# We's row in PSUM, and PE's side jobs behind each chunk's sums in a message-passing kernel on one Trainium2 core

## The reference

```python
xn = layernorm(x)
# 4 graph layers
for l in range(4):
    e   = edge_weight1 @ We[l] + be[l]              # (E,1) @ (1,D): one row We[l] times a number per edge
    m   = relu(h[src] + e)                          # a message per edge
    agg = segment_sum(m, dst, N)
    h   = ((1 + eps[l]) * h + agg) @ W1[l] + b1[l]
    h   = relu(batchnorm(h) * gamma[l] + beta[l])
    h   = relu(h @ W2[l] + b2[l])
# linear attention on the same xn
q, k, v = elu(xn @ Wq + bq) + 1, elu(xn @ Wk + bk) + 1, xn @ Wv + bv
kv = sum_s k v^T (per head);  z = 1 / (q . sum_s k)
mixed = (q kv z) @ Wp + bp
x = x + h + mixed
x = x + expert_ffn(layernorm(x))                    # top-1 of 8 experts
```

## Time and profile before

| what | value |
|---|---|
| median of 3 runs | 1772.68 us (1770.53 to 1775.09) |
| the profiled execution | 1772.85 us, of it 1771.1 us span |
| PE busy, x matmuls | 1462.0 us (83%) x6948 |
| DVE busy | 1310.3 us (74%) x2539 |
| POOL busy | 1081.7 us (61%) x1070 |
| ACT busy | 944.5 us (53%) x1086 |
| layer 0: start of POOL's first gather to the end of its last | 32.0 to 449.1 us |
| layer 1: relu of step 1 to relu of step 37 | 554.2 to 835.2 us |
| layer 2: the same | 933.0 to 1209.8 us |
| layer 3: the same | 1306.0 to 1583.8 us |

### The profile page before, as it was taken

The page is one execution under the profiler, slowest core; times in us unless marked ns, Lnnn a source line. Parts: engine busy times, 40 slices in busy tenths (PEclk is TensorE's granted clock), DMA queues, the critical chain, the costliest instruction groups (busy, mean ns, idle before and its releaser), DMA issues.

```text
span 1771.1 us, 22116 instructions
## 1 busy us (share of the span) xinstructions
PE 1462.0 (83%) x6948; PEld 645.9 (36%) x6948; DVE 1310.3 (74%) x2539; ACT 944.5 (53%) x1086; POOL 1081.7 (61%) x1070
## 2 busy tenths in 40 slices
PE   3767898867787888888888988889888898898797
PEld 2233344322333333333433333334433333334464
DVE  6788988978457887776586778776678878685634
ACT  3544544444245666665436667665456666673221
POOL 3777777777126777777047777773267777770033
PEclk8988999887999999999999999999999999999889
DMA  7776677677147777776257777783477777866343
GB/s 261 204 201 188 196 199 200 197 225 226 51 125 221 216 212 212 210 213 199 53 179 228 223 228 212 215 233 111 141 225 221 224 217 210 244 196 230 149 149 111
DMA packets 119094, 343.23 MB, mean 194 GB/s; under 512 B 20712, under 2 KB 24892, under 8 KB 118718
## 3 DMA queue, kind: packets, MB, share of 16 engines
q0 software_dynamic: 85248, 278.41, 55.0%
q1 hardware_dynamic: 32318, 60.78, 10.6%
q10 hardware_dynamic: 1408, 2.56, 0.4%
HBM read 323.61 MB, written 19.96 MB: 194 GB/s over the span
## 4 chain that ended last, share of the span: by engine, by line
PE 45%; DVE 16%; POOL 13%; ACT 12%; issue 8%; DMA 4%; DVEq 1%; POOLq 0%; ACTq 0%; SPq 0%
PE ps L1799 41%; POOL ring L817 13%; ACT ring L1593 10%; DVE ring L1006 8%; PE ps L1864 3%; DMA ring<-x_table,idxT 3%; DVE lg L1061 1%; DVE aggT L1421 1%; DVE onehot L1000 1%; DMA aggT<-pair_table,token_i 1%; DMA ring<-in_x 1%; DVEq L1048 0%; PE ps L2229 0%; DVE ring L940 0%; DVE aggT L1062 0%
## 5 line engine op out<-in xcount | busy, mean ns | idle before, releaser
L817 POOL DMA_INDIRECT ring<-x_table,idxT x1014 | 1039.3, 1025 | 514.4 <-issue 293.1
L1006 DVE SCALAR_TENSOR_TENSOR ring<-we_bc,wT,ring 128x512 f32<-128x512 f32 x1014 | 688.7, 747 | 63.6 <-DMA ring<-x_table,idxT 58.5
L1593 ACT ACTIVATE ring<-ring 128x3072 f32<-128x3072 f32 x161 | 444.7, 2762 | 282.9 <-DVE ring L1006 282.9
L1799 PE MATMUL ps<-ring,onehot 128*32 128x512 f32 x2028 | 360.2, 650 | 198.3 <-ACT ring L1593 194.5
L1639 ACT ACTIVATE zT<-ps 128x512 f32<-128x512 f32 x336 | 189.6, 601 | 145.6 <-PE ps L1799 142.7
L1799 PE MATMUL ps<-ring,zT 128*128 128x512 bf16 x1080 | 262.4, 382 | 0.8
L1799 PE MATMUL ps<-zT,xT 128*32 128x512 f32 (+2 forms) x752 | 256.5, 618 | 1.6 <-DVE mix L1195 1.6
L1061 DVE TENSOR_REDUCE lg<-ps 128x128 f32<-128x512 f32 x208 | 143.1, 688 | 118.0 <-PE ps L1864 72.2
L1799 PEld LDWEIGHTS ps<-ring,onehot 128*32 128x32 f32 x2028 | 72.3, 113 | 381.5 <-ACT ring L1593 242.9
L1799 PE MATMUL ps<-w,zT 128*125 128x512 f32 (+2 forms) x320 | 146.5, 621 | 20.2 <-ACT zT L1717 20.2
L1799 PE MATMUL ps<-aggT,w 128*128 128x512 f32 (+1 forms) x384 | 142.7, 522 | 6.9 <-DVE aggT L1062 3.6
(11 more groups left out here) (311 smaller groups left out, 1263.2 us busy)
## 6 DMA issues: line engine op xcount, KB each, us to landing
ring<-x_table,idxT POOLq DMA_INDIRECT x1014, 3.8
zT<-slot_table SPq DMA_DIRECT2D x36, 312.5 KB
w<-in_L_gnn_W SPq DMA_DIRECT2D x8, 1024.0 KB, 10.7
ring<-in_L_ffn_W SPq DMA_DIRECT2D x16, 512.0 KB, 9.8
x_table<-ring SPq DMA_DIRECT2D x24, 250.0 KB
x_table<-ring SPq DMA_DIRECT2D x9, 256.0 KB
stage<-in_x ACTq DMA_DIRECT2D x9, 256.0 KB
pair_table<-mix SPq DMA_DIRECT2D x9, 256.0 KB
```

The source lines that it names most:

```text
L817: gp.indirect_dma_start(out=to, out_offset=None, in_=table[:, :], in_offset=bass.IndirectOffsetOnAxis(ap=idx, axis=0)).then_inc(done, 16)
L1006: ins = v.scalar_tensor_tensor(out=at[:, u, :], in0=we_bc[:, :], scalar=wT[:, c, u:u + 1], in1=at[:, u, :], op0=ALU.mult, op1=ALU.add)
L1593: a.activation(at, at, ACT.Relu).then_inc(relu_done, 1)
L1799: return nc.tensor.matmul(o, lhsT, rhs, start=start, stop=stop)
```

## The change

1. **We's row in PSUM.** In layers 1 to 3 ACT copies `we_bc` into `ps[6]` (`terms_copy`, in `first_pieces`), in layer 0 into `ps[5]` at step 14, and DVE's edge terms read that bank in place of SBUF; layer 0 does so from step 15 on (`TERMS_FROM`).
2. **Banks.** `ps[6]` is no longer free in layers 1 to 3: the tiles rotate through two banks in all three layers (`TAKES = 2`), so `first` is 2 tiles in layers 2 and 3 too. `att` goes into `ps[7]`, the bank of `fold_picked`. The values of layer 0 go into `ps[7]`, kv into one bank as 8 matmuls of 64 rows x 65 columns a tile (4 of 129 columns before).
3. **Norms.** The attention's divisors are computed at the end of layer 0 (`norms`: 4 matmuls of 2 columns for each of 10 node tiles, at steps 47 to 51) and inverted there; `att` on DVE is one multiplication in place of two reciprocals and two.
4. **Order in layers 1 to 3.** On PE a step is now: `first` tiles, `group_sums` with `place_rows`, `fold_groups`, `fold_picked`, `later` tiles, side job, early sums. DVE and ACT look up the side job of step j-1 (`beside_of`), and DVE's `flush_picked` and statistics also come a step later. The fine steps are rearranged to match.

```diff
-    def takes(l):
-        return 2 if l == 1 else 3
+    TAKES = 2
...
-        return tiles[:takes(l)], tiles[takes(l):]
+        return tiles[:TAKES], tiles[TAKES:]
...
+    def beside_of(l, j):
+
+        return beside_at(l, j - 1)
...
+    TERMS_FROM = QS + 3
+    act_jobs[QS + 1].append(("terms", 0))
+
+    NORMS = ((46, range(0, 6)), (47, range(6, 7)), (48, range(7, 8)), (49, range(8, 9)), (50, range(9, NT)))
+    for at, tiles in NORMS:
+        pe_jobs[at] += [("norms", t) for t in tiles]
+    dve_jobs[51].append(("norms", 0))
...
+        def terms_bank(l):
+            return ps[6] if l in MIXED else ps[5]
...
+                terms = terms_bank(l) if l in MIXED or j >= TERMS_FROM else we_bc
+                if l not in MIXED and j == TERMS_FROM:
+                    v.wait_ge(terms_ready, 1)
                 for u in tiles:
-                    ins = v.scalar_tensor_tensor(out=at[:, u, :], in0=we_bc[:, :], scalar=wT[:, c, u:u + 1],
+                    ins = v.scalar_tensor_tensor(out=at[:, u, :], in0=terms[:, :], scalar=wT[:, c, u:u + 1],
                                                  in1=at[:, u, :], op0=ALU.mult, op1=ALU.add)
...
+            def terms_copy(l):
+
+                a.wait_ge(we_loaded, l * 16 + 16)
+                a.activation(terms_bank(l)[:, :], we_bc[:, :], ACT.Copy).then_inc(terms_ready, 1)
...
                 elif l in MIXED:
                     pe.wait_ge(pick_relu, QB[l + 1] * SW)
+                    pe.wait_ge(pick_out, QB[l + 1])
...
-                if at >= takes(l):
-                    pe.wait_ge(pick_relu, at - takes(l) + 1)
+                if at >= TAKES:
+                    pe.wait_ge(pick_relu, at - TAKES + 1)
...
+                    first, later = tiles_of(l, j)
+                    for T in first:
+                        take_rows(l, T)
+                    group_sums(l, j)
+                    for T in placed_at(l, j):
+                        place_rows(l, T)
+                    fold_groups(l, j - 1)
+                    if fold_at(j) is not None:
+                        fold_picked(l, fold_at(j))
+                    for T in later:
+                        take_rows(l, T)
                     beside(l, j)
                     early_sums(l, early_of(l, j))
-                    if fine_of(l, j) is not None:
-                        if l in MIXED and fold_at(j) is not None:
-                            fold_picked(l, fold_at(j))
-                        fine_sums(l, j)
-                        continue
-                    first, later = tiles_of(l, j) if l in MIXED else ([], [])
-                    for T in first:
-                        take_rows(l, T)
-                    if l in MIXED and fold_at(j) is not None:
-                        fold_picked(l, fold_at(j))
-                    group_sums(l, j)
-                    if l in MIXED:
-                        for T in placed_at(l, j):
-                            place_rows(l, T)
-                    fold_groups(l, j - 1)
-                    if l in MIXED:
-                        for T in later:
-                            take_rows(l, T)
...
+                if kind == "norms":
+                    r = rows(i)
+                    if i == 0:
+                        pe.wait_ge(v_ready, NT)
+                        pe.wait_ge(kvblk_ready, 1)
+                    for f in range(KD):
+                        at = i * NORM + f * 2
+                        ins = mm(v_bank[0:r, at:at + 2], mix[:, i, f * P:f * P + r], kvblk[:, f, P:], True, True)
                     ins.then_inc(nd_done, 1)
```

More of the change, by code:

```diff
@@ L191, in build_gps_block @@
                 order.append(("j", j - 2))
-            if l in MIXED and fold_at(j) is not None:
-                order.append(("q", fold_at(j)))
+            if l in MIXED and fold_at(j - 1) is not None:
+                order.append(("q", fold_at(j - 1)))
         assert len(order) == NC
@@ L1033, in add_fine @@
                     add_tiles(l, j, range(p * PAIR, (p + 1) * PAIR)).then_inc(last_summed, 1)
-                    if f == FINE - 1 and p == 1:
+                    if l in MIXED:
+                        if p == 0:
+                            flush(l, "j", j - 2)
+                            if f > 0:
+                                early_stats(l, early_of(l, j - 1))
+                        if p == 1:
+                            flush_picked(l, j)
+                            early_stats(l, early_of(l, j if f > 0 else j - 1))
+                    elif f > 0 and p == 1:
                         flush(l, "j", j - 2)
-                        if l in MIXED:
-                            early_stats(l, early_of(l, j))
                 if f == FINE - 1:
@@ L1040, in add_fine @@
                     flush(l, "j", j)
-                else:
+                elif l not in MIXED:
                     flush(l, "j", j - 2)
-                    flush_picked(l, j)
             def flush(l, kind, i):
@@ L1064, in flush_picked @@
             def flush_picked(l, j):
-                if l in MIXED and fold_at(j) is not None:
-                    flush(l, "q", fold_at(j))
+                if l in MIXED and fold_at(j - 1) is not None:
+                    flush(l, "q", fold_at(j - 1))
             def early_stats(l, e):
@@ L1093, in messages @@
             def messages(l):
-                v.wait_ge(we_loaded, l * 16 + 16)
+                if l in MIXED:
+                    v.wait_ge(terms_ready, l + 1)
+                else:
+                    v.wait_ge(we_loaded, 16)
                 if l in MIXED:
@@ L1110, in messages @@
                     beside(l, j)
-                    if l in MIXED:
-                        if ready_at(j) is not None:
-                            picked_ready(l, ready_at(j))
-                        if j < NJ[l] - 1:
-                            early_stats(l, early_of(l, j))
-                    else:
+                    if fine_of(l, j) is None or l not in MIXED:
                         early_stats(l, early_of(l, j - 1))
+                    if l in MIXED and ready_at(j) is not None:
+                        picked_ready(l, ready_at(j))
             def general(l):
@@ L1185, in beside @@
             def beside(l, j):
-                for kind, i in dve_jobs[j - 1] if l == 0 else beside_at(l, j):
+                for kind, i in dve_jobs[j - 1] if l == 0 else beside_of(l, j):
                     job(l, kind, i)
@@ L1720, in beside @@
             def beside(l, j):
-                for kind, i in act_jobs[j - 1] if l == 0 else beside_at(l, j):
+                for kind, i in act_jobs[j - 1] if l == 0 else beside_of(l, j):
                     if kind == "columns":
@@ L1854, in fine_sums @@
                 ins.then_inc(parts_done, 1)
-                fold_groups(l, j if f > 0 else j - 1)
+                if f > 0:
+                    fold_groups(l, j)
+                elif l not in MIXED:
+                    fold_groups(l, j - 1)
             def fold_groups(l, j):
@@ L2012, in key_value @@
                 for c in range(KD):
[L2013 to L2014 removed]
+                    for h in range(2):
+                        ins = mm(ps[6][h * HD:(h + 1) * HD, c * (HD + 1):(c + 1) * (HD + 1)], k_rows[0:r, c * P + h * HD:c * P + (h + 1) * HD],
+                                 v_rows[0:r, c, h, :], t == 0 and c == 0, t == NT - 1 and c == KD - 1)
                 ins.then_inc(kv_done, 1)
```

121 lines of the change are left out of this document (73 added, 48 removed).

## The result

The changed kernel takes 1825.06 us (median of 4 runs, 1824.27 to 1826.05) against 1773.88 us for the kernel before (median of 4, 1770.53 to 1779.96): a ratio of 1.029, 95% interval 1.027 to 1.032. It is slower by 51 us. The forecast was 1799 us and its range ended at 1811.

What follows compares the result with a forecast made beforehand. POOL was taken to bound layer 0, a loop of PE and ACT layers 1 to 3. Layer 0 -8, layer 1 +4.9, layer 2 +15.1 and layer 3 +14.0 made 1772.85 + 26 = 1799 us, range 1788 to 1811 (8 in 10: 1756 to 1811).

Steps and rivals of the forecast that it cites:

- What bounds the kernel: POOL's gathers pace layer 0 at 7.93 us a chunk; a loop of PE and ACT paces layers 1 to 3.
- The end of each layer (+2.8): Layers 1 to 3: last pair's relu 21.4 us after relu 37, against 18.64 before, +2.8 us a layer.
- Two banks in layers 2 and 3: Three steps take 23.10 or 24.41 us, not 23.64; first three +4.5 a layer, the rest +7.8 and +6.7.
- Rival B: Layers 2 and 3: the two banks cost nothing, each layer gives +5 to +6, 1781 us in all; chance 0.14.
- Fold_picked (+0.45 a turn): Layers 1 to 3: hidden before, it now stands inside the loop and adds 0.45 us a turn.
- Layer 0 (-8): Layer 0: 13 us gained by faster gathers less 5 us lost to the norms, -8 us in all.
- The gathers' pace: Layer 0 from step 15 on: 35 chunks at 7.57 us in place of 7.94, a gain of 13 us.
- the norms: End of layer 0: 10.5 us of PE work comes in, about 8 us are free, 5 us lost.
- Edge terms from PSUM at no price for DVE: DVE's edge terms: 745 ns with one operand in PSUM against 747 in SBUF, costed at 0.
- Rival C: Norms cost 10.5 us, or PSUM edge terms cost DVE 0.39 us a chunk where late: 1808 us; chance 0.09.
- Rival A: POOL paces layers 2 and 3 too, so faster gathers gain there: about 1744 us; chance 0.22.
- Rival D: Layer 0's gathers stay at 1.32 us, so layer 0 gives +5 in place of -8: 1812 us; chance 0.05.

Runs made afterwards that it cites:

- experiment 9: The changed kernel with DVE's statistics of the last early sums moved behind the last pair's edge terms: 1816.98 us, ratio 1.025.
- experiment 11: The changed kernel with one matmul in place of four in the early sum of step 37: 1814.97 us, ratio 1.023.
- experiment 12: The changed kernel with the edits of experiment 9 and experiment 11 together: 1799.06 us, ratio 1.015.
- experiment 6: The changed kernel with edge terms read from SBUF in layer 0 only: 1838.76 us, ratio 1.037.
- experiment 8: The changed kernel with layer 1 and layers 2 and 3 from step 34 in the old order, three banks and SBUF terms in layers 2 and 3: 1771.07 us.
- the executions listed above the experiments: Seven profiled executions sharing the changed kernel's layers 2 and 3: 290.3 us with one turn at the lower clock, up to 297.5 with four.
- experiment 1: The kernel before with two take banks in place of three in layers 2 and 3: 1793.95 us, ratio 1.012.
- experiment 3: The changed kernel with three take banks in layers 2 and 3 and edge terms from SBUF in layers 1 to 3: 1788.67 us, ratio 1.011.
- experiment 2: The changed kernel with `fold_picked` back ahead of the chunk's sums in layers 1 to 3: 1807.86 us, ratio 1.020.
- experiment 7: The changed kernel with one of the four norms matmuls of each node tile (10 in place of 40): 1818.11 us, ratio 1.026.
- experiment 13: Layer 0 of the changed kernel without the norms, `att` with two banks, layers 1 to 3 as in the kernel before: 1760.54 us, ratio 0.994.
- experiment 4: The changed kernel with edge terms from SBUF in layers 1 to 3, still two banks: 1831.67 us, ratio 1.031.

## Why the prediction was wrong

The direction, the stages and the loop of PE and ACT were right, and the sum was half of what came: 52.4 us against 26. Two steps of the forecast failed. The term for the end of a layer was too small by 12.2 us over the three layers. And the sum had no term for TensorE's lower clock, which makes most of the other 14.2: 4.7 in each of layers 2 and 3, 4.6 in layer 0 and 0.2 in layer 1.

- **What bounds the kernel.** Right: POOL in layer 0, and the loop of PE and ACT where there are two banks. Steps in layer 1 are 7.34, 7.34 and 8.4 us, as forecast. That its 283.2 us agree so well with 283.0 is in part luck: the first three steps took 22.2 us and not 23.8, because those of the kernel before held a turn at the lower clock, and one such turn (1.7 us) came later.
- **The end of each layer (+2.8): the term that failed most.** It is 6.2 to 7.2 us, 12.2 us more over three layers. The last pair came at 23.4 us and not at 21.4. The forecast ended the early sum of step 38 at 15.3 where PE ended it at 16.7, because small waits and the folds also stand on a full PE; the third ended at 21.3, and a last pair at 21.4 would have needed it at some 19.3. Experiments 9, 11 and 12 show what the 4.7 us against before are: 2.3 of DVE's statistics ahead of the last edge terms, the rest the sum of step 37. Behind the last pair come another 1.4 to 2.8 us, for which the forecast had nothing. In layer 1 most of them are 8.86 us for 32 matmuls of 128x226 that took 6.37 before, at a granted clock of 0.70. That is no mark of the new order: these matmuls took 6.37 us in experiment 6, with the new end, and 8.06 in layer 2 of experiment 8, with the old one.
- **Two banks in layers 2 and 3: right as a loop, with the clock left out.** The first three steps cost 5.3 us and not 4.5 (3.6 in executions where none of them had the lower clock); the other 33 came to 269.9 us and not 265.9. Each layer had three turns at the lower clock, 1.7 us each. Without them it is 288.6 us, and the forecast's loop gives 23.1 + 265.9 = 289.0. That each such turn is on the path is seen from the executions listed above the experiments. The kernel before has such sums as well (26 and 34 records over 0.8 us in layers 2 and 3, against 24 and 28); that other waits hide them there is argued and not shown. Rival B, that the banks cost nothing, falls with experiments 1 and 3.
- **Fold_picked (+0.45 a turn): right**, 0.44 in the chain, and 0.4 a turn in experiment 2. That its cost depends on the bank was not seen: with three banks none shows (experiment 3), and in the old order two banks cost 11 to 13 us a layer, in the new one 18 to 23.
- **Layer 0 (-8): -3.4 in this execution, -6.1 in the mean of the ten that have it (-1.2 to -11.3).** The gathers' pace was right (7.58 against 7.57 us a chunk), and so nearly were the norms (5 forecast, 5.7 between the two traces), though experiments 7 and 13 leave their size open and some 3 us of the 5.7 came without norms too. Most of what this execution missed is POOL's stop at step 15, 5.8 us in place of 2.5, where PE stayed at the lower clock. It is no wait that the change put in. The new wait for `left_known` ahead of the first `v` is 1.4 us in every execution with this layer 0 and stands behind the sums that POOL waited for. The stop was 4.9 to 7.0 us in the four of the ten where the side job ahead of the sums took 5.25 to 6.75 us, and 2.0 to 3.3 in the six where it took 3.70. What decides between the two stays open.
- **Edge terms from PSUM at no price for DVE: right** (743 against 746 ns, and experiment 4). Rival C's second half falls. Its first half, norms at 10.5 us, is not borne out here, with 5.7, but in experiment 2 the same stretch took 10.3 us more than in the kernel before.
- **Rivals A and D** are out. From 963 to 1233 us POOL waited 20 times for PE, 24.8 us, and three steps there took 24.5 us, not under 22.9. In layer 0 the gathers started 7.58 / 6 = 1.26 us apart, not 1.32.

## What to carry to other kernels

Before a buffer is given up for a faster transfer, ask whether it keeps one engine's work off another's loop. Here We's row in that PSUM bank bought nothing in layers 2 and 3, where POOL had time, and the missing bank cost 18 to 23 us in each. Work that fits under a wait costs nothing only there, so for each moved step ask under which wait it lay, and what lies on the path once it comes one step later; at a stage's end a shift by one step is one item more on the path. When two edits work on one loop, measure them apart and together. And before a few us between two executions are put down to a wait in the code, look at the granted clock of both in that stretch, and at the same stretch in executions that share it.

## What was not expected of the hardware

A DVE operation that reads one operand from PSUM in place of SBUF took as long (743 against 746 ns), while POOL's gathers beside it fell from 1010 to 956 ns in the mean (experiments 6 and 4). And the lower clock turned up in single steps of a loop that looks the same each turn, with 1.83 us of idle PE ahead of the sums in a slow turn and in a fast one alike: the sums of a step then took 4.4 us in place of 2.7. Which turns it hit differed between executions of the same layers. In layer 0, behind sums wholly or partly at the lower level in all of them, PE was back at the upper level for the side job that follows in six executions of ten and not in four, and POOL's stop was 2.0 to 3.3 us in the six and 4.9 to 7.0 in the four.
